# Attention on one Trainium2 core: row maxima by wide reads over two-bank score buffers, the diagonal's mask added by TensorE

## The reference

```python
scores = jnp.einsum('bqhd,bkhd->bhqk', Q, K) / math.sqrt(D_K)
causal = jnp.tril(jnp.ones((Sx, Sx), dtype=bool))
scores = jnp.where(causal, scores, -jnp.inf)
attn = jax.nn.softmax(scores, axis=-1)
out = jnp.einsum('bhqk,bkhd->bqhd', attn, V).reshape(Bx, Sx, N_HEADS * D_K)
```

## Time and profile before

| | us |
|---|---|
| Median of 3 runs | 1375.2 (1371.19 to 1381.31) |
| Profiled execution, first to last instruction (span) | 1440.9 |
| TensorE busy in the span | 1111.1 (77%) |
| VectorE busy | 853.0 (59%) |
| ScalarE busy | 674.2 (47%) |
| Attention, row maxima of the first group | 481 to 506 |
| Attention, groups | 512 to 1024 |

### The profile page before, as it was taken

The page is one execution under the profiler, slowest core; times in us unless marked ns, Lnnn a source line. Parts: engine busy times, 40 slices in busy tenths (PEclk is TensorE's granted clock), DMA queues, the critical chain, the costliest instruction groups (busy, mean ns, idle before and its releaser), DMA issues. The chain is left out here.

```text
span 1440.9 us, 28115 instructions
## 1 busy us (share of the span) xinstructions
PE 1111.1 (77%) x7114; PEld 671.0 (47%) x7117; DVE 853.0 (59%) x2530; ACT 674.2 (47%) x1676; POOL 463.3 (32%) x520
## 2 busy tenths in 40 slices
PE   3458988875786589999899899998694698897840
PEld 2246766664332134444334334443372577676630
DVE  5763333332884688888788788884177533333335
ACT  3513343332455056766666666666454243333320
POOL 3636666653234400000000000000165456665620
PEclk8558999998778589999999999999897599999975
DMA  7502222223586914555544444440273022222238
GB/s 244 182 1 81 82 79 80 83 77 103 179 262 173 167 16 61 78 74 78 73 60 60 61 60 61 72 57 9 84 232 110 19 75 84 80 81 75 76 122 264
DMA packets 130285, 141.06 MB, mean 98 GB/s; under 512 B 46800, under 2 KB 104592, under 8 KB 130192
## 3 DMA queue, kind: packets, MB, share of 16 engines
q1 hardware_dynamic: 116368, 102.24, 31.8%
q0 software_dynamic: 13824, 37.77, 8.3%
HBM read 86.88 MB, written 52.69 MB: 97 GB/s over the span
## 5 line engine op out<-in xcount | busy, mean ns | idle before, releaser
L1407 ACT ACTIVATE t_prob<-t_psS 128x512 f32<-128x512 f32 (+3 forms) x768 | 328.1, 494 | 189.1 <-PE t_psS L1339 155.6
L1427 DVE CUSTOM_DVE_ANT_0 t_psR<-t_psR,all_causal 128x128 f32<-128x128 f32 (+3 forms) x512 | 246.4, 505 | 60.4 <-PE t_psR L1317 52.9
L1317 PE MATMUL t_psR<-stacks_kst,stacks_qst 96*128 96x512 bf16 (+3 forms) x768 | 231.2, 345 | 29.3 <-PEq L886 20.3
L1336 PE MATMUL t_psS<-stacks_qst,stacks_kst 99*128 99x512 bf16 (+3 forms) x768 | 224.0, 329 | 2.7 <-ACT t_prob L1407 2.0
L1431 DVE TENSOR_REDUCE t_maxp<-t_psR 128x1 f32<-128x512 f32 x256 | 176.0, 688 | 21.1 <-PE t_psR L1317 20.3
L1350 PE MATMUL t_psO<-t_prob,t_vst 128*32 128x512 f32 (+3 forms) x1536 | 163.6, 498 | 3.0 <-ACT t_prob L1407 1.1
L1317 PEld LDWEIGHTS t_psR<-stacks_kst,stacks_qst 96*128 96x128 bf16 x768 | 70.1, 98 | 201.0 <-DVE t_maxp L1427 103.1
L1308 POOL COPY t_vst<-stacks_v_rows 128x512 f32<-128x512 f32 x16 | 9.9, 616 | 443.3 <-DMA stacks_v_rows<-v_rows 443.2
L670 PE MATMUL be_psG<-b_w,be_xT 128*128 x432 | 119.8, 413 | 13.0 <-issue 8.6
L670 PE MATMUL ae_psG<-a_w,ae_xT 128*128 x432 | 118.2, 408 | 14.3 <-issue 8.1
L763 DVE TENSOR_TENSOR ae_hid<-ae_sg,ae_psG 128x256 f32<-128x256 f32 x72 | 30.4, 422 | 139.1 <-ACT ae_sg L733 106.8
(11 more groups left out here) (284 smaller groups left out, 1901.1 us busy)
## 6 DMA issues: line engine op xcount, KB each, us to landing
qk_parts<-q_parts SPq DMA_DIRECT2D x32, 384.0 KB, 2.8
stacks_qst<-qk_parts SPq DMA_DIRECT2D x96, 128.0 KB, 4.7
stacks_kst<-qk_parts SPq DMA_DIRECT2D x96, 128.0 KB, 7.4
q_yk<-y_rows SPq DMA_DIRECT2D x16, 512.0 KB, 5.4
s_yk<-y_rows SPq DMA_DIRECT2D x16, 512.0 KB, 5.4
o_rows<-t_orow SPq DMA_DIRECT2D x32, 136.0 KB, 8.8
bl_raw<-o_rows SPq DMA_DIRECT2D x8, 544.0 KB, 4.0
xn_rows<-al_xn SPq DMA_DIRECT2D x8, 512.0 KB, 4.3
```

The costliest lines, as they stand in the source:

```text
L1317: nc.tensor.matmul(psR[bank][:, 0:w], qst[slot][0:KROWS, h, i * P:(i + 1) * P], kst[slot][0:KROWS, h, k0:k0 + w], start=True, stop=True).t ...
L1336: ins = nc.tensor.matmul(ps, kst[k][0:MROWS, h, j * P:(j + 1) * P], qst[k][0:MROWS, h, a:(c + 1) * 512], start=True, stop=a > j * P)
L1407: nc.scalar.activation(prob[j % 2][:, h, a:(c + 1) * 512], psS[n % ST_BANKS][:, a - c * 512:512], ACT.Exp, scale=DK ** -0.5).then_inc(exp_ ...
L1427: ins = nc.vector.tensor_tensor_reduce(psR[bank][:, 0:w], psR[bank][:, 0:w], T.causal[:, 512 - w:512], 1.0, -BIG, ALU.add, ALU.max, maxp[: ...
```

## The change

The ring becomes two slots of two banks each (`RING_SLOTS`, `RING_W`), and `psS` has two banks in place of three (`ST_BANKS`). A group has 22 units: one for query tile 0 (four heads of 128 keys side by side), one for tile 1 (four of 256), two each for tiles 2 and 3 (two heads, a bank each), four each for tiles 4 to 7 (one head, up to 1024 keys over both banks). After a unit's scores TensorE adds the mask on the diagonal blocks with the identity as weights, one matmul a bank that holds a diagonal. VectorE reads a unit with one reduction straight into `maxq`. The join is gone; the split has one instruction fewer. Both halves of the outputs are transposed in one slot, copied and stored at once. `AHEAD` is 5 units in place of 11, the outputs stand behind the third entry, and the plan reckons with other times.

```diff
-RING_BANKS = 3
-ST_BANKS = 3
-AHEAD = 11
-READER_LATENCY = 1000
+RING_SLOTS = 2
+RING_W = 1024
+ST_BANKS = 2
+AHEAD = 5
+OUT_AT = 3
+READER_LATENCY = 300
...
 def score_units():
...
+    for i in range(QT):
+        if i < 2:
+            units.append((i, 0, HG, (i + 1) * P))
+        elif i < QT // 2:
+            units += [(i, h, 2, 512) for h in range(0, HG, 2)]
+        else:
+            units += [(i, h, 1, RING_W) for h in range(HG)]
     return units
...
-        at = 4 if later else 0
-        ring[at:at] = [("o", c) for c in range(2)]
+        at = OUT_AT if later else 0
+        ring[at:at] = [("o",)]
...
-            kind, u = ring[n_ring][:2]
-            w = units[u][3] if kind == "s" else 512
-            t = start + w / 2.4
-            dve = max(dve, t + READER_LATENCY) + 64 + (w if kind == "s" else 900) * 1.04
-            ring_free[n_ring % RING_BANKS] = dve + 60
+            x = ring[n_ring]
+            t = start + made(x) / 2.4
+            dve = max(dve, t + READER_LATENCY) + 120 + read(x) * 1.04
+            ring_free[n_ring % RING_SLOTS] = dve + 60
...
-            def score(u, slot, r, bank):
-                h, i, k0, w, _ = units[u]
-                wait(pe, drained, r + 1 - RING_BANKS)
-                nc.tensor.matmul(psR[bank][:, 0:w], qst[slot][0:KROWS, h, i * P:(i + 1) * P],
-                                 kst[slot][0:KROWS, h, k0:k0 + w], start=True, stop=True).then_inc(filled, 1)
+            def score(u, stack, r, slot):
+
+                i, h0, n, pitch = units[u]
+                end, ps = (i + 1) * P, psR[slot]
+                wait(pe, drained, r + 1 - RING_SLOTS)
+                for h in range(n):
+                    for k0 in range(0, end, 512):
+                        w = min(end - k0, 512)
+                        nc.tensor.matmul(ps[:, h * pitch + k0:h * pitch + k0 + w], qst[stack][0:KROWS, h0 + h, i * P:end],
+                                         kst[stack][0:KROWS, h0 + h, k0:k0 + w],
+                                         start=(h * pitch + k0) % 512 == 0, stop=k0 + w < end)
+                in_bank = max(512 // pitch, 1)
+                for h in range(0, n, in_bank):
+                    diagonal = ps[:, h * pitch:(h + in_bank) * pitch].rearrange("p (n w) -> p n w", w=pitch)[:, :, i * P:end]
+                    ins = nc.tensor.matmul(diagonal, T.ident_bf[:], bc(T.causal[:], 1, [P, in_bank, P]), start=False, stop=True)
+                ins.then_inc(filled, 1)
+
+            def turn_max(r, slot):
+                pe.wait_ge(drained, r)
...
+            def turn_out(g, r, slot):
+                wait(pe, drained, r + 1 - RING_SLOTS)
+                pe.wait_ge(o_copied, g * 2 + 2)
+                for c in range(2):
+                    for i in range(512 // P):
...
                     if j == QHALF + 1:
+                        if with_before:
+                            act.wait_ge(drained, out_at(g - 1))
                         copy_out(g, 0)
                 copy_out(g, 1)
...
-                if k0 + w == (i + 1) * P:
-                    hold(dve, filled, r + 1, T)
-                    ins = nc.vector.tensor_tensor_reduce(psR[bank][:, 0:w], psR[bank][:, 0:w], T.causal[:, 512 - w:512], 1.0, -BIG,
-                                                         ALU.add, ALU.max, maxp[:, h, col:col + 1])
-                else:
-                    dve.wait_ge(filled, r + 1)
-                    ins = nc.vector.tensor_reduce(maxp[:, h, col:col + 1], psR[bank][:, 0:w], AX_X, ALU.max)
-                ins.then_inc(drained, 1)
-
-            def join_max(g, r):
-
-                dve.wait_ge(drained, r)
-                link(nc.vector.tensor_copy(maxq[:, :, 0:QHALF], maxp[:, :, 0:QHALF]), g, 1)
-                nc.vector.tensor_tensor(maxq[:, :, QHALF:QT], maxp[:, :, QHALF:QT], maxp[:, :, QT:QT + QHALF],
-                                        ALU.max).then_inc(max_ready, 1)
...
+                i, h0, n, pitch = units[u]
+                dve.wait_ge(filled, r + 1)
+                nc.vector.tensor_reduce(maxq[:, h0:h0 + n, i], psR[slot][:, 0:n * pitch].rearrange("p (n w) -> p n w", w=pitch)[:, :, 0:(i + 1) * P],
+                                        AX_X, ALU.max).then_inc(drained, 1)
...
-                nc.vector.tensor_scalar(neg[:], psR[bank][0:MROW, 0:P], -1.0, None, ALU.mult).then_inc(drained, 1)
+                link(nc.vector.tensor_scalar(mparts[:, 0], ps, -1.0, None, ALU.mult), g, 1)
+                nc.vector.scalar_tensor_tensor(mid[:], ps, -1.0, mparts[:, 0], ALU.mult, ALU.subtract).then_inc(drained, 1)
...
-    T.causal, T.causal_t = M.sb("causal", [P, 512]), M.sb("causal_t", [P, P], BF16)
+    T.causal, T.causal_t = M.sb("causal", [P, P], BF16), M.sb("causal_t", [P, P], BF16)
```

More of the change, by code:

```diff
@@ L1138, in plan_step @@
     if with_before:
-        at = 4 if later else 0
-        ring[at:at] = [("o", c) for c in range(2)]
+        at = OUT_AT if later else 0
+        ring[at:at] = [("o",)]
     st = [("st", j, c, h) for j in range(QT) for c in range(2) for h in range(HG) if width(j, c) > 0]
     pv = [("pv", j, c) for j in range(QT) for c in range(2) if width(j, c) > 0]
-    need_s = sum(units[x[1]][3] for x in ring if x[0] == "s") or 1
+    read = lambda x: (units[x[1]][0] + 1) * P * units[x[1]][2] if x[0] == "s" else 700
+    made = lambda x: read(x) + P * units[x[1]][2] if x[0] == "s" else 500
+    need_s = sum(read(x) for x in ring if x[0] == "s") or 1
     need_t = sum(width(x[1], x[2]) for x in st)
-    order, ring_free, st_free = [], [0.0] * RING_BANKS, [0.0] * ST_BANKS
+    order, ring_free, st_free = [], [0.0] * RING_SLOTS, [0.0] * ST_BANKS
     exp_end, pv_end = {}, {}
@@ L1288, in _ @@
             store_out(NG - 1)
[L1289 to L1290 removed]
+            sp.wait_ge(o_stored, 16 * NG)
         def heads(rows, width):
@@ L1313, in _ @@
         def _(pe):
-            def score(u, slot, r, bank):
-                h, i, k0, w, _ = units[u]
-                wait(pe, drained, r + 1 - RING_BANKS)
-                nc.tensor.matmul(psR[bank][:, 0:w], qst[slot][0:KROWS, h, i * P:(i + 1) * P],
-                                 kst[slot][0:KROWS, h, k0:k0 + w], start=True, stop=True).then_inc(filled, 1)
-            def turn_max(g, r, bank):
-                wait(pe, drained, r + 1 - RING_BANKS)
-                pe.wait_ge(max_ready, g + 1)
-                nc.tensor.transpose(psR[bank][0:MROW, 0:P], maxq[:].rearrange("p h i -> p (h i)"), T.ident[:]).then_inc(filled, 1)
@@ L1325, in turn_out @@
-            def turn_out(g, c, r, bank):
-                wait(pe, drained, r + 1 - RING_BANKS)
-                pe.wait_ge(o_copied, g * 2 + c + 1)
-                for i in range(512 // P):
-                    ins = nc.tensor.transpose(psR[bank][:, i * P:(i + 1) * P], oT[:, c, i * P:(i + 1) * P], T.ident[:])
+            def score(u, stack, r, slot):
[13 more added lines that the diff above has]
+                ins.then_inc(filled, 1)
@@ L1364, in step @@
                         continue
-                    r, bank = base + idx, ring_bank(g, idx)
+                    r, slot = base + idx, ring_slot(g, idx)
                     if what == "s":
@@ L1371, in step @@
                             asked = True
-                        score(u, (k + ahead) % SLOTS, r, bank)
+                        score(u, (k + ahead) % SLOTS, r, slot)
                     elif what == "m":
-                        turn_max(g + 1, r, bank)
+                        turn_max(r, slot)
                     else:
-                        turn_out(g - 1, at[0], r, bank)
+                        turn_out(g - 1, r, slot)
                     idx += 1
@@ L1453, in copy_rows @@
                 dve.wait_ge(filled, r + 1)
-                wait(dve, o_stored[c], g * 16)
-                nc.vector.tensor_copy(orow[:, c], psR[bank][:].rearrange("p (x w) -> p x w", w=VW)[:, :, 0:OW]).then_inc(drained, 1)
+                wait(dve, o_stored, g * 16)
+                nc.vector.tensor_copy(orow[:], psR[slot][:].rearrange("p (x w) -> p x w", w=VW)[:, :, 0:OW]).then_inc(drained, 1)
             def step(g, k, later, with_before):
                 base = ring_base(g)
-                for idx, (what, at, *_) in enumerate(plan_step(units, later, with_before)[1]):
-                    r, bank = base + idx, ring_bank(g, idx)
+                for idx, (what, *at) in enumerate(plan_step(units, later, with_before)[1]):
+                    r, slot = base + idx, ring_slot(g, idx)
```

98 lines of the change are left out of this document (42 added, 56 removed).

## The result

The change made the kernel slower: 1458.36 us (median of 4 runs, 1457.7 to 1459.44) against 1376.02 (4 runs of before beside it), a ratio of **1.0597 (95% interval 1.0569 to 1.0624)**, +82.3 us. The forecast was 1448 in 1390 to 1478. Of the executions reported here one is in the slow state and left out of its ratio (2649 us, with AHEAD 15 and the plan's latency alone, in the third set).

The account below looks back on a forecast made before the run. TensorE's queue was taken as the bound, 29.1 us of work and 2.9 of waiting a group. 15 groups at +4.9, -3 for the opening and +3 for the last group gave +73 on 1375.2: 1448 us, range 1390 to 1478.

Parts of the forecast that it names:

- Score banks: Transposed scores with two banks in place of three: new waits of 3.3 us in a group's tail plus 1.1 in earlier rounds.
- The walk: Step through the planned order behind O(4,1) with measured hand-overs: 0.52 and 0.21 us lost, 0.73 a round at 384 wide.
- Masks: Row maxima's masks on TensorE, 27 matmuls a group: +1.8 us straight onto the bound engine, at most +4.5 with gaps.
- Slot waits: Row-maxima ring of two slots: TensorE finds its slot still being read at six units, 1.5 us a group.
- Maxima chain: Joins and a copy go before the maxima's transpose: TensorE's wait there falls from 1.3 to about 0.1 us a group.
- The group's sum: Attention's steady group, work and waits added: 29.1 + 1.8 + 0.1 + 3.3 + 1.1 + 1.5 = 36.9 us against 32.0.
- Wide reads: VectorE's 22 row-maxima reads: 1.05 ns a column, 0.15 us fixed, 1.23 us at 1024, 22.7 us a group.
- The opening: Attention's start, VectorE's alone: 24.3 us become 21 with a later first read, so -3 us.
- The holes: Rival: TensorE's idle holes fill, without a new wait, making the kernel faster at 1355 us; chance 0.08.
- Half the waits: Rival: only 3 us of bank and slot waits a group, 1405 us; chance 0.09 for no change, needing under 1.9.
- The clock: Rival: TensorE's granted clock drops for one 4 us stretch in each group, costing 1.1 us, 1464 us; chance 0.08.
- VectorE as the bound: Rival: VectorE binds the group; its wide reads take 22.7 to 26 of 32 us, so no; chance 0.02.

Follow-up runs that it names:

- AHEAD 15 and the plan's latency alone: Kernel before with AHEAD 15 and the plan's reader latency 1150 in place of 1000, the maxima's transpose unmoved; ratio 0.9966 against before.
- the third set: Runs of before with three score banks: maxima's transpose later, plan numbers changed, or both, the last also with masks on TensorE; before took 1439.15 us there.
- the reordered queue: Kernel before with the maxima's transpose four ring entries later, AHEAD 15 and reader latency 1150; 1421.75 us beside 1439.15 of before, ratio 0.9879.
- the second trace of after: The changed kernel, unedited, traced again on another chip; 1461.98 us, ratio 1.0634 against before on that chip.
- later transpose: Kernel before with the maxima joined where they were but their transpose three ring entries later; ratio 0.9956 against before.

## Why the prediction was right, point by point

**The bound: right.** TensorE's queue set the group before, and does after. VectorE's busy time fell by 4.2 us a group and the group grew by 5.0.

**Score banks: the mechanism right and shown, the size nearly so.** New waits of 3.3 + 1.1 = 4.4 a group were predicted. In the steady groups after, the waits ahead of scores are 3.8, and with those inside the scores' masks and ahead of the accumulations some 4.1. Alone the two banks were expected at 3.5 to 4 net and cost 4.2 in a steady group. The walk was right to 0.01 us in the round shown above and to 0.03 in the two behind it, since it was made of hand-overs that the last group of before had shown. The sign that was named, TensorE waiting for ScalarE by 3 to 5 us a group, shows as 2.0 of idle time only (18.2 + 4.6 over 11.4 groups): a matmul's recorded end hides part of each wait, as 0.52 lost reads 0.36. The Trainium skill (Perfetto Trace Analysis, Optimization Strategy) says that consistent bubbles, the same gap over and over on the engine that should be saturated, can mean that there isn't enough SBUF or PSUM for the next tile. The trace agrees: 55 waits for `prob`, none over 0.5 us, mean 0.33, where before had none.

**Masks: the term right, their price alone about half of it.** 1.8 a group predicted; they occupy 1.9 in every kernel that has them. But added to a kernel they cost 0.7 to 0.9 of a steady group (alone in before, in after, and on the reordered queue), because the waits that were there become shorter by 1.1 to 1.2 us. The forecast's sum is not hurt by that: it took all of before's waits out and put the new ones in. "Straight onto the bound engine" is wrong as the price of one edit.

**Slot waits: right in size.** 1.5 predicted; 1.6 ahead of units after. Before had 0.8 there as well, with three banks: the prediction put all of before's 1.6 of short waits down to the score banks. Half of them stood in the ring. Taking the waits away by short reads gains 1.1 of a steady group.

**Maxima chain: right as a wait, worth less than it looked.** 1.3 to 0.1 predicted; 21.2 us became 2.4. But with three banks and everything else kept, taking this wait away gave 4.0 us in the phase, 0.3 a group: half of it came back as ring waits.

**The group's sum: 36.9 predicted, 37.0 measured, and not by luck.** Each term is within 0.3 us of what the steady groups show: own work with masks and gaps 30.9 (some 31.1), score banks 4.4 (4.1), slots 1.5 (1.6), maxima 0.1 (0.1). The same sum gives wrong prices for single parts, since waits on one queue stand in for each other: the score banks alone cost 4.2 and the masks alone 0.7, both together 4.7, and everything else in the change, wide units, slots, join and order, adds 0.3.

**Wide reads: right.** 1.23 us at 1024 predicted, 1.220 measured; the end in which each bank pays its fixed part is out. 22.7 us of reads a group predicted, 22.6 measured (22 of mean 1026 ns). With what overlaps and the rest of its work VectorE is busy 23.3.

**The opening: this step failed, in sign.** -3 was predicted, for reads that overlap as before. From the first row-maxima matmul to the first transposed score it took 31.2 us before (481.0 to 512.2) and 32.3 after (445.6 to 477.8). Up to the transpose of the maxima it was 24.7 (to 505.7) and is 25.2 (to 470.75); from there on 6.5, and now 7.1. Two windows of after in the first part, and VectorE's timeline there (the last reads of the group):

```profile
446.00:458.00 12.00, 10.76 (x43) 4.40 (x40) 10.04 (x11) 0.81 (x1) 11.66 (x7) 0.50 1.01 130
458.00:470.00 12.00, 10.59 (x32) 2.81 (x30) 11.31 (x12) 0.00 (x0) 2.93 (x5) 0.50 1.15 137
```

```profile
465.88 4.82 DVE L1439 TENSOR_REDUCE t_maxq<-t_psR 128x1 f32<-128x1024 f32 x4 [0.23 <-PE t_psR L1328]
```

VectorE is busy 10.04 and 11.31 of 12, as predicted, but the four reads take 4.82, 1.205 each beside a duration of 1.220: some 0.02 of overlap and not 0.1, and 0.2 to 0.6 of idle time stands between runs of them. The overlap had been read from a masked reduction followed by its accumulator's read-out, and was carried to plain reductions. What was also missed is what stands behind the reads. In the kernel whose reads are cut to 128 columns the split of the maxima starts 14.8 us behind the first matmul (449.2 to 464.0) in place of 25.6 (445.6 to 471.2), and yet the first transposed score starts 30.1 behind it, only 2.2 less than in the second trace of after (32.3). TensorE then waits for the load of the maxima's rows, start, us, and in the bracket 10.11 us of idle time:

```profile
478.29 1.01 PE L1322 MATMUL t_psR<-stacks_kst,stacks_qst 96*128 96x512 bf16 x2 [10.11 <-DMA stacks_qst<-t_mparts]
```

That load was issued by 467.7, behind the loads of later groups' stacks. So reads shortened by 11 us move the opening by 2; 3 us was more than the opening had to give, whatever the reads did. In after itself the first transposed score shows no wait for that load. TensorE's clock was 0.50 (1.2 GHz) in the opening before as well as after.

**The last group:** +4.2 where +3 was predicted. **The loop's turn:** +3.6 of idle time and 4.4 in all, not foreseen; it is told under what the runs showed of the hardware.

**The total:** +73 predicted, +82.3 measured. Missing are 4.4 at the turns, 4.1 in the opening, 1.2 in the last group and some 1.5 in the groups, about 11; attention differs by 84.0 in the traces and the times by 82.3. The steady group was close, and what lay around it all went the same way.

**The rivals.** The holes did not fill: fillers that are spread as well as was tried still leave groups of 34.6. Half the waits: no, 5.7 us of bank and slot waits and not 3. The clock, 1464 by its sum, lies nearer to the measured time than the forecast does, but its mechanism isn't there: the granted clock of the group's window is 1.00, and 0.98 over 560 to 980, which holds the two turns (before 1.00); in each group it would have needed a stretch below. At the turns it did fall, which is part of their 4.4. The Trainium skill (TensorE: Matmul & The Clock Gate, A second HAM failure mode: psum-queue depth-cycling) has the clock oscillate where TensorE often idles briefly between groups of matmuls; gaps of 0.3 to 0.5 us many times a group did not do it here. VectorE as the bound: no, by the shortened reads.

## What to carry to other kernels

An engine that hands banks to another should be costed with the number of banks as a term of its own: walk the order with the measured hand-overs (+0.26 and +0.05 us here), and a bank taken away shows as the same small loss in every round, here 4.2 us of a 32 us group. Air for an engine that is not the bound (VectorE, 4.2 us a group) doesn't pay for instructions or banks taken from the one that is. A part that is added to a bound queue costs less than it occupies while there are waits in that queue, even waits too short to show as idle time. If one instruction waits at the head of the bound queue, first try to move it a few entries back: that alone was worth 0.4%, with the plan fitted to it 1.2%, and the rewrite lost 6%.

## What the runs showed of the hardware

**The turn of a loop changed hands where masks stood on TensorE.** TensorE's idle time at the two turns was 1.97 and 2.01 us before, 3.71 and 3.92 after. It went with the row-maxima masks on TensorE in every kernel: 3.57/3.42 with the masks alone, 3.52/3.95 with masks and two banks, 3.50/3.79 in the third set; without them 2.58/2.65 (two banks), 2.31/2.20 (the change without masks), 1.90/1.90 (later transpose), 2.54/2.44 (four later, AHEAD 15) and 2.67/2.40 (the plan alone). What TensorE waits for differs too. Without the masks it passes the turn with a gap of some 0.2 us, works on, and then waits for VectorE or ScalarE, whose own turns take 2.2 to 3.2 us in which nothing is seen that they wait for ("issue"). In before:

```profile
703.72 0.39 PE L1317 MATMUL t_psR<-stacks_kst,stacks_qst 96*128 96x512 bf16 x1 [0.20 <-issue]
...
706.26 0.70 DVE L1427 CUSTOM_DVE_ANT_0 t_psR<-t_psR,all_causal 128x512 f32<-128x512 f32 x1 [2.29 <-issue]
```

**A reduction over two PSUM banks costs what its columns cost:** 1220 ns at 1024, 818 at 640, 1.05 ns a column across the border of the banks.

**A load in the queue's tail can hold the next bound.** The maxima's rows, 8 KB a load, landed some 12 us after their issue in the opening with short reads, behind stacks of 128 to 256 KB. In the opening of after, where they are issued later, it was 2.3 us (median).

**Waits on a busy queue can be too short to see.** In the reordered kernel TensorE is busy 29.97 of 30.00 us, and some 0.9 us a group of waits ahead of row-maxima units is still in it, by the matmuls' starts.
